# The output stage of a fused sequence layer: the residual add out of PSUM on VectorE, the token mean from one half-sum made by GpSimd

## The reference, cut to what matters

```python
def _ln(x, g, b, eps):
    mu = x.mean(-1, keepdims=True)
    var = ((x - mu) ** 2).mean(-1, keepdims=True)
    return (x - mu) / jnp.sqrt(var + eps) * g + b
...
    step: ... return ((W1n, b1n), xq + _ln(Z1_bar, g, bb, EPS_IN))   # 64 chunks of 16 tokens, one after the other
...
    return _ln(out, post_w, post_b, EPS_IN) @ o_w.T
```

## Time and profile before

| | us |
|---|---|
| median of 3 runs | 648.58 (648.12 to 648.94) |
| the profiled execution's own time | 648.52 |
| its span, first to last instruction | 646.7 |
| busy: TensorE / VectorE / ScalarE / GpSimd | 505.0 / 475.5 / 358.8 / 341.7 |
| the output stage: second mean (block 1) to last statistics | 504.1 to 569.4 |
| first product of the second layer | 575.6 |

### The profile page before, as it was taken

How to read it: one execution, slowest core, us unless ns; L and a number is a source line. 1 busy time by engine, 2 the same in 40 slices (tenths; PEclk the granted TensorE clock), 3 DMA queues, 4 the chain that set the end, 5 groups by cost and what they waited for, 6 DMA issues and landing times. The chain is left out here.

```text
span 646.7 us, 30020 instructions
## 1 busy us (share of the span) xinstructions
PE 505.0 (78%) x12294; PEld 360.2 (56%) x12294; DVE 475.5 (74%) x1488; ACT 358.8 (55%) x1170; POOL 341.7 (53%) x596
## 2 busy tenths in 40 slices
PE   0399999985488878787788887888687499859994
PEld 0144444444377777777777777777675244346652
DVE  6467777785479998899989898998997357527442
ACT  0344543334366777667767688767675277533521
POOL 1259999993245555555555555555653556420442
PEclk9999999996555555555555555555555699969998
DMA  9101111127600000000000000000004200000113
GB/s 343 70 0 46 42 45 34 32 57 160 129 5 1 1 1 1 2 0 1 1 1 1 0 1 2 0 1 1 0 4 186 101 1 0 2 2 1 67 66 130
DMA packets 10082, 24.77 MB, mean 38 GB/s; under 512 B 1988, under 2 KB 2728, under 8 KB 9768
## 3 DMA queue, kind: packets, MB, share of 16 engines
q1 hardware_dynamic: 10024, 24.09, 12.2%
HBM read 11.50 MB, written 4.19 MB: 24 GB/s over the span
## 5 line engine op out<-in xcount | busy, mean ns | idle before, releaser
L803 PE MATMUL PS<-work 32*32 32x32 f32 x4064 | 84.4, 238 | 60.0 <-DVE work L977 50.6
L803 PEld LDWEIGHTS PS<-work 32*32 32x32 f32 x4064 | 80.5, 152 | 70.8 <-issue 67.9
L792 PE MATMUL PS<-work 64*32 64x64 f32 x2048 | 69.5, 310 | 17.6 <-ACT work L1120 14.8
L1057 POOL TENSOR_TENSOR work<-work 128x128 f32<-128x128 f32 x64 | 25.5, 399 | 87.0 <-DVE work L977 75.8
L792 PEld LDWEIGHTS PS<-work 64*32 64x32 f32 x2048 | 55.7, 164 | 24.5 <-issue 23.0
L815 PE MATMUL PS<-work 32*64 32x32 f32 x2016 | 68.3, 292 | 1.3 <-issue 1.3
L815 PEld LDWEIGHTS PS<-work 32*64 32x64 f32 x2016 | 59.7, 216 | 5.4 <-issue 1.4
L510 PE MATMUL PS<-X,work 128*128 128x512 f32 x128 | 58.1, 598 | 0.1
L1049 POOL TENSOR_TENSOR work<-work,mask 128x256 f32<-128x256 f32 x64 | 46.6, 727 | 14.0 <-ACT work L1152 8.5
L1033 POOL TENSOR_TENSOR work<-KP,cst 128x256 f32<-128x256 f32 x64 | 39.2, 612 | 19.9 <-DVE work L936 16.8
L1152 ACT ACTIVATE work<-PS,small 128x128 f32<-128x128 f32 x64 | 23.5, 367 | 40.9 <-PE PS L792 40.9
(11 more groups left out here) (156 smaller groups left out, 1267.0 us busy)
## 6 DMA issues: line engine op xcount, KB each, us to landing
X<-in_x SPq DMA_DIRECT2D x4, 1024.0 KB, 8.0
TK<-KP SPq DMA_DIRECT2D x64, 64.0 KB, 1.9
X<-QP SPq DMA_DIRECT2D x8, 512.0 KB, 9.6
TK<-in_x SPq DMA_DIRECT2D x4, 1024.0 KB, 9.3
out<-TK SPq DMA_DIRECT2D x16, 256.0 KB, 2.4
work<-in_rope SPq DMA_DIRECT2D x2, 512.0 KB, 9.1
cst<-in_consts SPq DMA_DIRECT2D x1, 289.0 KB, 4.9
work<-in_wk SPq DMA_DIRECT2D x1, 256.0 KB, 11.2
```

Source lines behind the costliest of these rows:

```text
L792: mm = nc.tensor.matmul(PS[HD * a:HD * a + HD, ZB[p], b * ZW:b * ZW + ZW], KT2[p][r:r + 64, k * B + b, :, :].rearrange("p e t -> p (e t)") ...
L803: mm = nc.tensor.matmul(PS[HD * a:HD * a + HD, bank, b * width:b * width + HD], AM[p][HD * a:HD * a + HD, b, part, :, :].rearrange("p e t ...
L1057: nc.gpsimd.tensor_tensor(ZN, ZQ[p], bc(sdq[1 - p]), ALU.mult).then_inc(q["zn"], 1)
```

## The change

- The residual moves from GpSimd to VectorE, which adds PSUM bank 2+m straight onto `KN`. It is the first thing in `statistics(i-1)`, behind the centering of block i+2 and the reciprocal for block i+1. ScalarE's copy is gone, and so is GpSimd's add.
- TensorE's projection now waits for the semaphore of VectorE's add (`s_x1`) in place of that of ScalarE's copy (`s_oc`).
- GpSimd adds the two channel halves of each block into the place in `X` that `pre` has just read (`pool_sum2`, L343), and the mean is one matrix product in place of two. Each such sum waits for the mean of the block before.
- The statistics of block 5 move ahead of the last scaling.

```diff
@@ layer_norm(..., presum=None)
-                nc.gpsimd.tensor_tensor(sums[0], tile(i, 0), tile(i, 1), ALU.add).then_inc(q["add"], 1)
+                nc.gpsimd.tensor_tensor(sums[0] if sums else presum(i), tile(i, 0), tile(i, 1), ALU.add).then_inc(q["add"], 1)
...
-                if sums:
+                if sums or presum:
                     pe.wait_ge(q["add"], i + 1)
-                    nc.tensor.matmul(PS[:, 0, :], mean_c, sums[0], start=True, stop=True
+                    nc.tensor.matmul(PS[:, 0, :], mean_c, sums[0] if sums else presum(i), start=True, stop=True
                                      ).then_inc(q["mean"], 1)
@@ TensorE, project
                         if not first:
-                            pe.wait_ge(s_oc, (i - 1) * J + m + 1)
+                            pe.wait_ge(s_x1, (i - 1) * J + m + 1)
@@ VectorE
+                def residual(i):
+
+                    dve.wait_ge(s_xr[ORDER[i] // PER], 16)
+                    for m in range(J):
+                        dve.wait_ge(s_o, i * J + m + 1)
+                        nc.vector.tensor_tensor(blk_of(KN[:, m, :], ORDER[i]), blk_of(KN[:, m, :], ORDER[i]),
+                                                PS[:, 2 + m, :], ALU.add).then_inc(s_x1, 1)
+
                 def statistics(i):
 
+                    residual(i)
                     for m in range(J):
...
                 dve_invert(dve, NBLK - 1)
+                statistics(NBLK - 3)
                 dve_scale(dve, NBLK - 1)
-                for i in range(NBLK - 3, NBLK):
+                for i in range(NBLK - 2, NBLK):
                     statistics(i)
@@ GpSimd
                     if c == PRE_AT:
                         pre(0)
+                        pool_sum2(pool, 0, True)
...
-                def residual(i):
-                    pool.wait_ge(s_xr[ORDER[i] // PER], 16)
-                    for m in range(J):
-                        pool.wait_ge(s_oc, i * J + m + 1)
-                        nc.gpsimd.tensor_tensor(blk_of(KN[:, m, :], ORDER[i]), blk_of(X[:, m, :], ORDER[i]),
-                                                blk_of(KN[:, m, :], ORDER[i]), ALU.add).then_inc(s_x1, 1)
-
...
                         pre(1)
+                        pool_sum2(pool, 1, False)
                 pre(2)
+                pool_sum2(pool, 2, False)
                 pre(3)
-                for i in range(NBLK - 4):
-                    pre(i + 4)
-                    residual(i)
-                for i in range(NBLK - 4, NBLK):
-                    residual(i)
+                for i in range(3, NBLK):
+                    pool_sum2(pool, i, False)
+                    if i + 1 < NBLK:
+                        pre(i + 1)
@@ ScalarE
-                def output(i):
-
-                    for m in range(J):
-                        act.wait_ge(s_o, i * J + m + 1)
-                        nc.scalar.activation(blk_of(X[:, m, :], ORDER[i]), PS[:, 2 + m, :], ACT.Copy
-                                             ).then_inc(s_oc, 1)
-
                 def follow(i):
-                    if i > 0:
-                        output(i - 1)
```

More of the change, by code:

```diff
@@ L319, in has, with layer_norm @@
             return not isinstance(i, int) or i + n < NBLK
-        def layer_norm(tag, src, sq, sd, eps, w, b, scale, spread_bank, ready=None, sums=None, at=None):
+        def layer_norm(tag, src, sq, sd, eps, w, b, scale, spread_bank, ready=None, sums=None, at=None, presum=None):
             q = {n: sem(f"{tag}_{n}") for n in ("in", "mean", "xc", "sq", "var", "sd", "rs", "wide", "xh", "xn", "add",
@@ L339, in pool_sum @@
                 pool.wait_ge(s_k0, 2)
-                pool.wait_ge(q["in"], there)
+                pool.wait_ge(ready or q["in"], there)
                 if not first:
                     pool.wait_ge(q["mean"], mean)
-                nc.gpsimd.tensor_tensor(sums[0], tile(i, 0), tile(i, 1), ALU.add).then_inc(q["add"], 1)
+                nc.gpsimd.tensor_tensor(sums[0] if sums else presum(i), tile(i, 0), tile(i, 1), ALU.add).then_inc(q["add"], 1)
             def pool_sum_squares(pool, i, first):
@@ L736, in build @@
         q2, ot, act_a, pe_mean, dve_center, act_square, pe_var, act_sd, dve_invert, pe_widen, \
-            dve_scale, act_affine, _, _ = \
+            dve_scale, act_affine, pool_sum2, _ = \
             layer_norm("ln2", TT, sq, sd, eps6, "post_w", "post_b", gain,
-                       4, ready=s_pre, at=ORDER)
+                       4, ready=s_pre, at=ORDER, presum=lambda i: blk_of(X[:, 0, :], ORDER[i]))
         with nc.Block() as block:
@@ L1245, in _ @@
                     follow(i)
-                output(NBLK - 1)
             @block.sync
```

## The result

The changed kernel takes 663.39 us (median of 4 runs, 661.9 to 664.75); the kernel before took 648.35 beside it. The ratio is 1.023, 95% interval 1.0201 to 1.026: slower.

A forecast was written before the change was run, and what follows sets the result against it. The prediction took the output stage as bound by TensorE, 6.55 us per block. Terms 1.1 - 0.3 - 0.9 + 6.2 + 1.6 = +7.7, plus 4.8 for clock, gave +12.5 on 648.52: 661.0 us, range 655 to 665.5.

The forecast's parts named there:

- The bound moves from TensorE's work to its wait: Steady output stage: TensorE waits 2.45 us for VectorE's add, 8.1 us per block for 6.55, +6.2 over four cycles.
- The new add costs what the centering costs: Output stage, VectorE: the first new add takes 0.68 us, read from the centering; bounds 0.60 and 1.29.
- The clock: Output stage: TensorE's clock falls in every second of eight cycles, four falls at 1.2 us each, +4.8 us.
- Chunk 56: Scan: a third GpSimd add in this chunk holds up VectorE, +1.1 us, at most 1.24.
- Drain: At half clock, up to the mean of block 2: shorter means against two added half-sums, together -0.3 us.
- The mean of block 2: From this mean to that of block 3: 7.76 us in place of 8.63, -0.9, the clock rising after 4.1.
- The add comes in time: Rival, output stage: VectorE's add is done before the variance ends, 5.65 us per block, 644.0 us; chance 0.06.
- The clock holds: Rival, output stage: the wait comes but costs TensorE no clock, 656.2 us, range 654.5 to 658; chance 0.27.

The follow-up runs named there:

- e8_add_second: The changed kernel with VectorE's add moved between the centering and the reciprocal: 652.18 us, ratio 1.0048 to the kernel before.
- e1_add_first: The changed kernel with VectorE's add moved to the head of its turn, ahead of centering and reciprocal: 643.89 us, ratio 0.9913 to the kernel before.
- e4_filler: The changed kernel with two unread products per block on TensorE between variance and projection: 657.44 us, ratio 1.0124 to the kernel before.
- e7_filler1: The changed kernel with one unread product per block on TensorE between variance and projection: 657.73 us, ratio 1.0156 to the kernel before.
- e3_add_only: The changed kernel without GpSimd's half-sums, the mean again two products, VectorE's add kept: 667.73 us, ratio 1.0286 to the kernel before.

## Why the prediction was right

The forecast was 661.0 in a range of 655 to 665.5, the measured median 663.39. What decides it came as foreseen and was tested: the wait, its length, and that it costs clock. The smaller terms did not all come, and the number of falls was right by luck. In the sum of the table +12.5 was forecast and +16.0 measured.

- *The bound moves from TensorE's work to its wait.* The cycle was forecast at 8.1 and is 8.04; the idle time in it at 2.45, and the view shows 2.30 (it counts the last product's drain as busy). e8_add_second and e1_add_first move the add and get the cycles that the same sum gives.
- *The new add costs what the centering costs.* The pair takes 1.22, and one alone at the stage's end 0.69, for the 0.68 taken from the earlier trace rows. The pair at 547.91 has a GpSimd add beside it from 548.64 on and takes 1.22 all the same.
- *The clock.* Four falls were forecast and four came, but the working was off twice. It counted eight cycles and a fall in every second; there are six waits, and four had a fall. The price of one was mis-sized: 1.2 us was taken, 6.4 / 4 = 1.6 was paid, near the upper bound of 1.7. The falls come behind the wait, so the half-clock stretch lies on the projection, where TensorE has nothing but work. What decides which wait is followed by a fall was not found.
- *Chunk 56.* 0.9 for 1.1, by way of L977 alone. GpSimd's sum takes 1.33 there, so its full length was not paid.
- *Drain.* +0.5 in place of -0.3, a miss of 0.8. Of it 0.3 came before the mean of block 0 began (498.42 - 496.45 = 1.97, less the 1.7 above), with no cause looked for. The two half-sums cost 1.40 and 1.39 in place of 1.22 each, in good part because GpSimd starts them 0.13 after the adds that they wait for (0.15 in the rows of chunk 56 above), and the price was taken as that of adds without such a wait. The shorter mean of block 1 gave back 1.70 in place of 1.84.
- *The mean of block 2.* The gain from its shorter run was lost, because the clock rose later: 5.8 us after TensorE began at 516.94, where the prediction took 4.1 from the kernel before, so that nearly all of the first projection half of block 0 (3.37 in place of 1.98) ran at half clock. Nothing shows this to be a cost of the change: e4_filler and e7_filler1, whose code does not differ from the changed kernel's up to the mean of block 3, have the rise 3.1 and 6.0 us after the same mean's start, and take 7.19 and 8.64 for the stretch. (By its own 4.1 the prediction's 1.22 of projection at half clock should be 1.12; that moves its sum by 0.05.)
- *The rivals.* "The add comes in time" was priced at 644.0, with the point that decides named as its place before the centering. e1_add_first has it there and takes 643.9. The mechanism is that rival's; the fit to 0.1 is luck in part. Its four cycles give 3.4 for the 3.6 counted, but up to the mean of block 3 it loses 1.75 in place of a gain of 0.1, and the end (547.92 to 565.26) gains 2.4 in place of 0.8. "The clock holds" was priced at 656.2; e4_filler shows that case at 657.4.

The runs of the changed kernel lie 2.8 us apart, 661.9 to 664.75. The forecast 661.0 is under the lowest of them. Only one of them has a trace, so whether they differ in their number of falls is not shown.

## What to carry to other kernels

When a drain of PSUM moves to another engine, its cost is less its own duration than all that stands ahead of it in that engine's order. Add up the chain from the producer's last instruction through the new engine's queue to the producer's restart, and compare it with the producer's own cycle, before looking at busy shares. An idle time that this opens on TensorE can cost nearly as much again in clock (here 6.4 beside the 7.5 that the stage loses at full clock); and a two-line move in the order may be the whole difference between a loss of 2.3% and a gain of 0.9%.

## What the hardware showed that I had not expected

- TensorE's clock held at 1.00 with a rest of 1.25 to 1.49 us in every cycle of 7.2 to 8.0 (e7_filler1, e8_add_second, 41 us each). With waits of 2.11 to 2.30 it fell behind some and not behind others: four of six in the changed kernel, three of six in e3_add_only.
- With the same code before it, the clock rose from half to full 3.1 us after the mean of block 2 began in one run and 6.0 in another (e4_filler, e7_filler1).
- Work that nobody reads made the changed kernel faster by 6 us (663.39 to 657.44 by the medians). The spans of the two profiled runs, 662.5 and 655.0, differ by 7.5, of which 1.35 is the earlier rise just named.
